# A Mamba block's scan and the entry of a five-stage transformer kernel: jobs at other units, the first rows in two transfers

## The reference

```
x = x + 0.5 * moe(layernorm(x))       # stage 1: 16 experts, top 6, and a shared SwiGLU
x = x + mamba(layernorm(x))           # stage 2: the selective scan
x = x + 0.5 * moe(layernorm(x))       # stage 3
x = x + 0.5 * hadamard_ffn(layernorm(x))   # stage 4
x = x + attention(layernorm(x))       # stage 5
x = x + 0.5 * hadamard_ffn(layernorm(x))   # stage 6
```

```
h, gate = split(x @ W_in.T)
u   = silu(causal_conv4(h) + conv_b)
ts, B, C = split(u @ Wx.T); each RMS-normed
delta = softplus(ts @ Wdt.T + dt_bias)
s[i,n] = exp(delta[i] * A[i,n]) * s[i,n] + delta[i] * B[n] * u[i]   # over t
y[i]   = sum_n s[i,n] * C[n] + D[i] * u[i]
out = (y * silu(gate)) @ Wout.T
```

## Time and profile before

| what | value |
|---|---|
| median of 3 runs | 1901.24 us (1899.95 to 1901.25) |
| the profiled execution | 1902.52 us, its span in the trace 1900.7 us |
| entry, until PE's first projection | 12.84 us |
| scan, first to last | 495.4 us to 967.2 us |
| DVE busy from 494 to 968 us | 455.64 of 474 us |
| mean granted clock of PE | 0.993 of full |

### The profile page before, as it was taken

How to read it: one execution, slowest core, us unless ns; L and a number is a source line. 1 busy time by engine, 2 the same in 40 slices (tenths; PEclk the granted TensorE clock), 3 DMA queues, 4 the chain that set the end, 5 groups by cost and what they waited for, 6 DMA issues and landing times.

```text
span 1900.7 us, 26241 instructions
## 1 busy us (share of the span) xinstructions
PE 1808.4 (95%) x9417; PEld 1375.2 (72%) x9417; DVE 1333.8 (70%) x1870; ACT 945.2 (50%) x1782; POOL 581.2 (31%) x399
## 2 busy tenths in 40 slices
PE   7999999999799999988689999999999999999998
PEld 6888888888354544534267888888888887777887
DVE  6666656567999999999976666565675556666533
ACT  3442323333688677684445433233333338888422
POOL 1000234000489878888720000000000025555000
PEclk9999999999899999999999999999999999999999
DMA  5332344220222222223202233232121306553100
GB/s 197 90 98 66 97 145 136 64 62 23 67 73 70 69 72 77 71 71 108 72 17 76 72 95 105 65 104 63 64 77 44 65 1 147 109 109 68 37 12 23
DMA packets 84186, 146.39 MB, mean 77 GB/s; under 512 B 13848, under 2 KB 23704, under 8 KB 83544
## 3 DMA queue, kind: packets, MB, share of 16 engines
q1 hardware_dynamic: 84056, 144.72, 26.6%
HBM read 130.38 MB, written 14.29 MB: 76 GB/s over the span
## 4 chain that ended last, share of the span: by engine, by line
PE 72%; DVE 14%; issue 6%; ACT 4%; POOL 3%; DMA 0%; DVEq 0%; SPq 0%; POOLq 0%; ACTq 0%
PE psum L161 19%; PE psum L162 18%; PE psum L163 18%; DVE scan_state L1618 6%; PE psum L1437 5%; POOL scan_state L1208 2%; PE psum L1990 1%; PE psum L1361 1%; DVE scan_state L1625 1%; PE psum L1332 1%; ACT attn_p L2138 1%; DVE X L807 1%; DVE moe_hidden_lo L850 1%; PE psum L1421 1%; PE psum L278 1%
## 5 line engine op out<-in xcount | busy, mean ns | idle before, releaser
L1208 POOL TENSOR_TENSOR scan_state<-scan_delta_u,scan_B_rows 128x1024 f32<-128x1024 f32 x127 | 299.5, 2368 | 95.3 <-PE psum L1437 81.2
L161 PE MATMUL psum<-xnT_hi,moe_w_hi 128*128 128x512 f32 x800 | 316.5, 396 | 2.7 <-DVE xnT_lo L470 2.6
L778 ACT ACTIVATE moe_hidden<-psum 128x512 f32<-128x512 f32 x200 | 119.5, 597 | 393.9 <-PE psum L163 393.9
L162 PE MATMUL psum<-xnT_lo,moe_w_hi 128*128 128x512 f32 x800 | 314.2, 393 | 0.0
L163 PE MATMUL psum<-xnT_hi,moe_w_lo 128*128 128x512 f32 x800 | 312.0, 390 | 0.0
L1618 DVE TENSOR_TENSOR_SCAN scan_state<-psum,scan_state 128x1024 f32<-128x1024 f32 x128 | 292.2, 2283 | 4.2 <-POOL scan_state L1208 3.0
L827 DVE TENSOR_TENSOR moe_gated_up<-moe_gate_rows,psum 128x512 f32<-128x512 f32 x184 | 126.5, 688 | 210.0 <-PE psum L163 124.8
L1437 PE MATMUL psum<-scan_state,ident 128*128 128x512 f32 x512 | 248.1, 608 | 3.8 <-DVE scan_gated L1633 2.6
L418 POOL TENSOR_SCALAR rstd<-mean_var 128x2 f32<-128x2 f32 x48 | 10.5, 220 | 752.8 <-DVE mean_var L452 752.5
L161 PE MATMUL psum<-moe_w_hi,moe_hidden_hi 128*128 128x256 f32 x800 | 230.4, 288 | 3.9 <-DVE moe_hidden_lo L850 2.6
L163 PE MATMUL psum<-moe_w_hi,moe_hidden_lo 128*128 128x256 f32 x800 | 226.3, 283 | 0.0
(11 more groups left out here) (226 smaller groups left out, 3476.4 us busy)
## 6 DMA issues: line engine op xcount, KB each, us to landing
scan_B_rows<-scan_B SPq DMA_DIRECT2D x127, 256.0 KB, 3.1
moe_gate_rows<-gate_table SPq DMA_DIRECT2D x176, 128.0 KB, 3.0
moe_w_raw<-moe_pack SPq DMA_DIRECT2D x50, 384.0 KB, 4.0
attn_stack<-attn_rows SPq DMA_DIRECT2D x96, 128.0 KB, 5.3
moe_gate_rows<-gate_table SPq DMA_DIRECT2D x32, 224.0 KB, 3.1
ffn_w_raw<-ffn_pack SPq DMA_DIRECT2D x16, 384.0 KB, 3.6
moe_gate_rows<-gate_table SPq DMA_DIRECT2D x32, 160.0 KB, 2.6
moe_gate_rows<-gate_table SPq DMA_DIRECT2D x24, 192.0 KB, 2.8
```

Of the source, the lines that this page charges most:

```text
L161: e.matmul(out, wH, xH, start=start, stop=False)
L162: e.matmul(out, wH, xL, start=False, stop=False)
L778: e.activation(self.hb[:, b, :], self.k.psum[:, 2 * b, :], ACT.Silu).then_inc(self.s_silu.sem, 1)
L1208: e.tensor_tensor(self.st[q % self.NBUF][:], self.dtu[:, 2 * h:2 * h + 2, :], self.Bs[:, q % self.RING, :].unsqueeze(1).broadcast_to([P, 2 ...
```

## The change

- The first chunk's rows come in two transfers of 256 rows, each with a semaphore; DVE waits for the second only in front of the second half's statistics.
- ACT splits the first weight tile before the two high halves of the entry, and the second tile after both (before: one after each half). DVE puts the low weights and both low halves in front of the statistics of the next rows.
- At the gates' units (n = 0, but not the very first) PE does the job after the spread and before the sums, and so before it waits for the gate.
- `out1` goes from unit 10 to 6 and its add from 12 to 8; `v1` from 6 and 7 to 8 and 9; `h2`, `h3` from 8, 9 to 10, 11. `g2` goes from 25 to 19, `g3` from 26 to 25, the next but one chunk's `h0` from 29 to 26 and `h1` from 30 to 29. In chunk 0 `g0`, `g1` go from 10, 11 to 6, 7. The diagonals 2 and 3 go from unit 19 to 20 and 21.

```diff
@@ Tail
         if entry:
+            self.s_in2 = Sem(k, "in0b")
             self.s_in = [Sem(k, f"in{c}") for c in range(NCH)]
...
         if self.entry:
             e.wait_ge(self.s_in[c].sem, self.s_in[c].at(16))
+            if c == 0 and p:
+                e.wait_ge(self.s_in2.sem, self.s_in2.at(16))
@@ Entry
     def chunk(self, e, c):
+        if c == 0:
+            for p, sem in enumerate((self.tail.s_in[0], self.tail.s_in2)):
+                e.dma_start(self.k.X[:, 2 * p:2 * p + 2, :],
+                            self.x[p * 2 * P:(p + 1) * 2 * P, :].rearrange("(n p) f -> p n f", p=P)
+                            ).then_inc(sem.sem, 16)
+            return
...
     def scalar(self, e):
+        self.moe.split_hi(e, 0)
         for p in range(2):
             self.tail.act(e, 0, 2 * p + 1)
-            self.moe.split_hi(e, p)
+        self.moe.split_hi(e, 1)
...
             t.norm(e, 0, q)
+        self.moe.split_lo(e, 0)
+        t.low(e, 0, 0)
+        t.low(e, 0, 1)
         t.add(e, 1, 0)
         t.stats(e, 1, 0)
-        t.low(e, 0, 0)
-        self.moe.split_lo(e, 0)
-        t.low(e, 0, 1)
@@ Scan
-    JOBS = {0: ("dt2", 0), 1: ("dt3", 0), 2: ("out0", -1), 4: ("v0", 1, 0), 5: ("v0", 1, 1), 6: ("v1", 1, 0),
-            7: ("v1", 1, 1), 8: ("h2", 1), 9: ("h3", 1), 10: ("out1", -1), 12: ("v2", 1, 0), 13: ("v2", 1, 1),
+    JOBS = {0: ("dt2", 0), 1: ("dt3", 0), 2: ("out0", -1), 4: ("v0", 1, 0), 5: ("v0", 1, 1), 6: ("out1", -1),
+            8: ("v1", 1, 0), 9: ("v1", 1, 1), 10: ("h2", 1), 11: ("h3", 1), 12: ("v2", 1, 0), 13: ("v2", 1, 1),
             14: ("v3", 1, 0), 15: ("v3", 1, 1), 16: ("xp0", 1, 0), 17: ("xp0", 1, 1), 18: ("ms0", 1),
-            20: ("dt0", 1), 21: ("dt1", 1), 22: ("xp1", 1, 0), 23: ("xp1", 1, 1), 24: ("ms1", 1),
-            25: ("g2", 0), 26: ("g3", 0), 27: ("g0", 1), 29: ("h0", 2), 30: ("h1", 2), 31: ("g1", 1)}
-    START = {2: ("h0", 1), 3: ("h1", 1), 10: ("g0", 0), 11: ("g1", 0)}
-    DIAG = {0: (0,), 1: (1,), 19: (2, 3)}
+            19: ("g2", 0), 20: ("dt0", 1), 21: ("dt1", 1), 22: ("xp1", 1, 0), 23: ("xp1", 1, 1), 24: ("ms1", 1),
+            25: ("g3", 0), 26: ("h0", 2), 27: ("g0", 1), 29: ("h1", 2), 31: ("g1", 1)}
+    START = {2: ("h0", 1), 3: ("h1", 1), 6: ("g0", 0), 7: ("g1", 0)}
+    DIAG = {0: (0,), 1: (1,), 20: (2,), 21: (3,)}
...
             if n == 0 and q:
                 e.wait_ge(self.s_z.sem, self.s_z.at(q + 1))
                 spread(q + 1)
+                if self.job(q):
+                    job(self.job(q), self.BANK)
                 e.wait_ge(self.s_yg.sem, self.s_yg.at(2 * c + h))
...
-            if self.job(q):
+            if self.job(q) and (n or not q):
                 job(self.job(q), self.BANK)
...
-            if c and r in (4, 12):
+            if c and r in (4, 8):
                 add(c - 1, 0 if r == 4 else 1)
```

## The result

The changed kernel takes 1912.76 us (median of 4 runs, 1911.68 to 1913.73) where the kernel before takes 1901.24 (median of 4 runs here, 1899.95 to 1901.96). The ratio estimated from the single runs is 1.0053, 95% interval 1.0041 to 1.0066. It is slower, as forecast, but by 10.1 us by the ratio (7.8 to 12.5) and 11.5 us by the medians, where 4.1 were forecast, and outside the range.

What follows compares the result with a forecast made beforehand. PE was taken to bound the feed-forward stages and DVE the scan. Terms -1.9 + 1.4 + 2.1 + 3.0 - 0.5 = +4.1 us on the 1901.24 us median gave 1905.3 us; range 1898 to 1908 us.

Steps and rivals of the forecast that it cites:

- Start: Entry: two transfers and statistics behind the low halves let PE start sooner; -1.9 us (-0.9 to -2.6).
- Chunk 0: Gate rows at units 6 and 7: PE waits for ACT's silu of g1, passed whole to DVE; +1.4 us.
- Jobs in front of the sums at gates' units: Unit 0 of chunks 1 to 3: dt2 waits for g1's silu, delaying the sums; two clock drops in three; +2.1 us.
- rival (d): Gates' units: longer gaps give three clock drops; +1.6 us on the forecast, 1906.9 us; chance 0.15.
- rival (a): Gates' units: dt2 breaks the gap, so the clock does not fall; -3.1 us, 1902.2 us; chance 0.17.
- Gate rows and diagonals: Units 19 to 25: unit 23's sum ends about 1.0 us later, delaying POOL's train to three borders; +3.0 us.
- Rival (b): POOL's and chunk 0's delays are hidden: sum 23 no later, g1 read in time; -4.4 us, 1900.9 us; chance 0.15.
- Second output: Output at unit 6, add at 8: the add waits 1.0 us instead of 1.31; -0.5 us (-2.6 to 0).
- Rival (c): Border waits and second add's wait go, the start gives 2.6; -9.3 us, 1891.9 us; chance 0.15.

Runs made afterwards that it cites:

- start alone: The kernel before with only the entry's edits (two transfers, first weight split ahead, low halves ahead of the next statistics): 1902.06 us, ratio 0.9998.
- first-half moves: The kernel before with only `out1` and its add, `v1`, `h2`, `h3` and chunk 0's `g0`, `g1` moved: 1902.91 us, ratio 0.9994.
- second-half moves: The kernel before with only `g2`, `g3`, `h0`, `h1` and the diagonals 2 and 3 moved: 1908.21 us, ratio 1.0023.
- diagonals alone: The kernel before with only diagonals 2 and 3 moved from unit 19 to 20 and 21: 1906.42 us, ratio 1.0011.
- job in front: The kernel before with only PE's job put ahead of the sums at both gates' units: 1909.73 us, ratio 1.0033.
- border without the stall: The kernel before with the entry's edits, the job ahead of the sums, and `g1` and `h1` exchanged at units 30 and 31: 1901.16 us, ratio 0.9986.

## Why the direction was right and the size wrong

**Start: right.** PE's first projection was forecast at about 11 us. PE's timeline of the entry after the change:

```profile
11.17 0.77 PE L161 MATMUL psum<-xnT_hi,moe_w_hi 128*128 128x512 f32 x1 [1.46 <-DVE xnT_lo L473]
```

That is 1.67 us ahead of 12.84, and at the scan 1.6 are left (1.9 in the run of the start alone). The first statistics start 0.99 us sooner (4.38 for 5.37), where 0.85 was taken for the two transfers; the new order of DVE gives the other 0.7 of the 1.05 forecast. The clock rose sooner by about as much, which the term had allowed for: PE's matmuls of 512 columns go from 0.63 to 0.39 us at 16.0 us before and at 14.4 after.

**Chunk 0: right.** +1.5 for +1.4, at the place forecast; the run of the first-half moves alone gives the same 1.45 us. The whole of it is one weighing (533.88, shown above). PE's timeline after has the wait that causes it, 0.92 us for 1.1 in the text:

```profile
531.56 1.99 PE L1342 MATMUL psum<-scan_conv_in,scan_taps 128*128 128x512 f32 x4 [0.92 <-ACT scan_silu_gate L1506]
```

**Jobs in front of the sums at gates' units: the step that failed, by its size.** The mechanism is what the text said: dt2 waits for the silu of g1, the sums wait for dt2, and the clock falls. The size was "+2.1 us", from "I keep two drops in three", and it measured +5.5. Split by first eights: the stall is worth 0.7 to 0.85 us a border (32.18 against 31.33 and, in chunk 3, 33.06 against 32.34 in the runs with a low clock and no stall), 2.4 in sum, as forecast (0.8 each); the drop at the border that had been spared, chunk 2, 1.7; and a low stretch at chunk 3's border that lasted for twice as long (857.6 to 864.4 us), 1.5 more (34.53 against 33.06). "PE stands longer in front of this work than before" stood in the text as a reason, and I did not let it change the count; that a stretch could last twice as long I had not thought of. Over all profiled executions of this study the borders come out so:

| order at the border | executions | borders with a low clock |
|---|---|---|
| job in front of the sums, stall of about 1.5 us for g1's silu | 3 | 9 of 9 |
| sums in front, g1 last | 7 | 13 of 21 |
| job in front of the sums, h1 last: no stall | 4 | 1 of 12 |

This is what rival (d) described (three drops), and rival (a), that dt2 breaks the gap, holds only once dt2 need not wait. That the stall, with the clock behind it, causes the loss at the borders is shown: the edit alone brings both, exchanging two jobs takes both away, with and without the other moves. What each of them costs is only worked out from the first eights, since no border had the stall and a full clock.

What stays open is when a gap is followed by a low clock. With the sums in front, the second-half moves alone and the diagonals alone had it at all three borders, the former with a longer gap (1.40 for 0.91), and both with a lower mean clock over ten runs. But the changed kernel with its sums in front has those moves too and had one drop, the kernel before had two, and the first-half moves alone none. The Trainium skill ("TensorE: Matmul & The Clock Gate", What's actually happening) has the clock follow recent busyness and vary between runs. By that, these observations fit; the traces agree in so far as gaps alike ended either way (13 low of 21, and in chunk 3 a gap of 2.26 us low, one of 2.30 not).

**Gate rows and diagonals: right in place, too high in size.** +2.4 for +3.0. POOL's timeline at unit 23 and after it shows the step as forecast: it waits for the sum and then runs without a gap up to the train that begins with scan 0's state.

```profile
586.22 2.35 POOL L1218 TENSOR_TENSOR scan_state<-scan_delta_u,scan_B_rows 128x1024 f32<-128x1024 f32 x1 [1.61 <-PE psum L1449]
...
609.92 9.32 POOL L1218 TENSOR_TENSOR scan_state<-scan_delta_u,scan_B_rows 128x1024 f32<-128x1024 f32 x4
```

Scan 0 waits 1.40 to 1.43 us for POOL, ACT's 0.37 in front of scan 31 is gone, and scan 30 waits 0.38 to 0.47 us for POOL instead. The two make 1.8 to 1.9, the lower end of the 1.9 to 2.4 forecast for one wait. The step was the delay of unit 23's sum, put at 1.0 us: the border moved by 0.8. By runs, the diagonals give 0.4 a border, the other second-half moves 0.1, and the jobs in front of the sums the remaining 0.3 (29.73, 29.75 and 29.66 with the sums in front, 30.19, 29.92 and 29.84 without; in chunk 0 it is one weighing's wait of 0.52 us, at 588.44), though on the kernel before they lengthen these units by nothing (29.25, 29.12). Rival (b), all this hidden, did not hold.

**Second output: right in two chunks.** The add waits 1.14 us for the 1.0 forecast, and units 8 to 15 are 0.17 us shorter in chunks 1 and 2, -0.3 us for the -0.5 forecast. But in chunk 3 a further stretch at the low clock, from 885 us, lies on the output: its add waits 1.80 us where 0.1 stood, and the units take 1.7 more. I had no term for it. The three other traces with this output at unit 6 don't have it, so nothing ties it to the move.

**Behind the scan: no term, +1.9 us.** The changed kernel's trace has a low stretch at 1592 us, in the attention stage, where the kernel before has none. Ten of the fourteen profiled executions of this study have one to three between 1560 and 1620 us, under kernels that are the same in that stage. From the last scan's start to the end the four without one take 935.5 to 936.2 us, those with one or two 936.7 to 938.7, the one with three 940.2. So no edit of the change makes this difference. Whether the other three runs of the changed kernel had such a stretch is not known.

**What the miss is made of.** The trace is 7.0 us over the forecast's +4.1. The gates' units have 3.4 of it, the second output 1.9, what lies behind the scan 1.9, the start and chunk 0 0.4, and the gate rows and diagonals -0.6. Nearly all of it, 6.8 us, is low clock that the forecast did not have: a third drop (1.7), the one that lasted twice as long (1.5), the one on the second output (1.7) and the one in attention (1.9). The failed step alone, put right, would have given 1908.7 us.

**Do the parts make the whole?** The ratios of start (0.9998), first-half moves (0.9994), job in front (1.0033) and second-half moves (1.0023) multiply to 1.0048; the change as a whole has 1.0053 (1.0041 to 1.0066). Rival (c), faster, failed where the text said: POOL's work has no gap in front of the border.

## What to carry to other kernels

Before a job is put in front of a wait, look at who reads the buffer that it writes and when: work that is put into a gap of PE, but itself waits, makes the gap longer (0.64 us in front of the sums became 1.49 in front of dt2), and in the trace the low clock took more than the wait did. With the same job in front, a predecessor that is read early gave 8.7 us back by the ratio. And where two engines run in step, look for the one piece that is longer than the beat (an output of 16 matmuls, one small subtraction of POOL ahead of the product that the scan needs): splitting it or letting it go one place later gave 0.22% and 0.15%, the latter seen in the traces only.

## What the runs showed of the hardware

- A wait of 1.49 us on top of 0.87 to 1.38 us (with 0.5 us of matmul between) was followed by a granted clock of 0.50 nine times in nine; gaps of 0.87 to 1.40 us with the sums in front 13 times in 21.
- The cost of a low clock depends on where the stretch lies. One under unit 0's sums and dt2 (616.8 to 620.2 us in the kernel before) costs DVE 1.7 us (31.33 for 29.65): PE is still behind when the first output, 16 matmuls in 3.62 us, comes in unit 2. The one in chunk 3 of the border without the stall begins earlier, at the spread (848.9 us), and costs 0.7 (31.37 for 30.66). A second one in chunk 3 of the kernel before, from 876.2 to 879.6 us, where no output comes behind it, costs nothing that can be measured: this first eight is 32.34 us, 1.7 over 30.66, as with one stretch.
- The first rows in two transfers brought the first statistics from 5.37 to 4.38 us. With the new order the entry won 1.6 us at scan 0 in the mean of seven traces against seven, and nothing that the medians of 10 and 26 runs can tell (0.9998, 0.9989 to 1.0008): the spread between executions of one kernel, 1901.1 to 1906.4 us in the last group, is larger.
